# A transformer block on one core: TensorE's local program padded to whole blocks of 256 instructions, shorter packets for a value copy, new step orders

## The reference

```python
def attn_layer(x, Wqkv, qs, ksc, Wo):
    qkv = x @ Wqkv
    q, k, v = jnp.split(qkv, 3, -1)
    ...
    q = l2norm(q) * qs
    k = l2norm(k) * ksc
    ...
    q = q * cos * scale + rotate_half(q) * sin * scale
    k = k * cos * inv + rotate_half(k) * sin * inv
    out = local_attention(q, k, v)      # windows of 32: own and previous, softmax
    return out @ Wo

def ffn_layer(x, g, bln, W1, b1, W2, b2):
    ...
    a, gate = jnp.split(xn @ W1 + b1, 2, -1)
    return a * jax.nn.gelu(gate, approximate=False) @ W2 + b2
...
for i in range(DEPTH):                  # 6
    x = attn_layer(shift_tokens(x), Wqkv[i], q_scale[i], k_scale[i], Wo[i]) + x
    x = ffn_layer(shift_tokens(x), ln_g[i], ln_b[i], W1[i], b1[i], W2[i], b2[i]) + x
```

## Time and profile before

| | |
|---|---|
| median of 3 runs | 3510.96 us (3510.58 to 3515.58) |
| span of the profiled execution | 3495.1 us |
| local stage, first to last `lb` | 799.7 to 3467.5 us |
| PE busy | 3309.7 us (95%) |
| POOL busy | 2907.1 us (83%) |
| DVE busy | 2951.4 us (84%) |
| ACT busy | 2468.4 us (71%) |
| DMA queues' share | 40.9% |

### The profile page before, as it was taken

How to read it: one execution, slowest core, us unless ns; L and a number is a source line. 1 busy time by engine, 2 the same in 40 slices (tenths; PEclk the granted TensorE clock), 3 DMA queues, 4 the chain that set the end, 5 groups by cost and what they waited for, 6 DMA issues and landing times.

```text
span 3495.1 us, 158019 instructions
## 1 busy us (share of the span) xinstructions
PE 3309.7 (95%) x69988; PEld 1936.2 (55%) x69988; DVE 2951.4 (84%) x3104; ACT 2468.4 (71%) x3349; POOL 2907.1 (83%) x2483
## 2 busy tenths in 40 slices
PE   7999999779999999999999999999999999999997
PEld 4666666445555555555555555555555555555553
DVE  6888888688888988888888889888998889988873
ACT  5777777556777767777677777676877777767764
POOL 3665555588999989999899999898999999989993
PEclk9999999999999999999999999999999999999997
DMA  1000000154645545545455454555554554545452
GB/s 67 5 5 5 5 5 5 44 119 102 143 114 130 120 115 126 131 112 127 113 126 127 106 137 110 129 120 121 120 135 105 142 124 109 140 108 134 102 124 62
DMA packets 163861, 347.33 MB, mean 99 GB/s; under 512 B 32876, under 2 KB 42352, under 8 KB 153840
## 3 DMA queue, kind: packets, MB, share of 16 engines
q1 hardware_dynamic: 163184, 337.23, 40.9%
HBM read 24.62 MB, written 4.19 MB: 8 GB/s over the span
## 4 chain that ended last, share of the span: by engine, by line
PE 70%; DVE 11%; POOL 6%; issue 6%; ACT 4%; SPq 2%; DMA 1%; DVEq 0%; POOLq 0%; ACTq 0%
PE psA L697 29%; PE psB L697 23%; PE psB L559 8%; PE psA L559 6%; PE psB L754 3%; DVE h L1338 3%; DVE pt L1237 1%; SPq L490 1%; PE psA L754 1%; DVE negm L1342 1%; DVE sum L1349 1%; DVE ts L1330 1%; DVE h L1320 1%; DMA kf<-h 1%; POOL sq L1443 1%
## 5 line engine op out<-in xcount | busy, mean ns | idle before, releaser
L1410 POOL TENSOR_TENSOR pt<-wk,pt 128x256 f16<-128x256 f32 (+3 forms) x256 | 368.1, 1455 | 288.7 <-ACT pt L939 199.0
L1443 POOL TENSOR_TENSOR sq<-sq 128x512 f32<-128x512 f32 x384 | 488.5, 1281 | 79.6 <-ACT sq L1022 78.2
L1438 POOL TENSOR_TENSOR h<-h,ts 128x512 f32<-128x512 f32 x384 | 499.8, 1302 | 1.2 <-DVE ts L1330 1.2
L1439 POOL TENSOR_TENSOR h<-h,ts 128x512 f32<-128x512 f32 x384 | 497.1, 1295 | 0.0
L1338 DVE TENSOR_TENSOR h<-h,psB 128x1024 f32<-128x1024 f32 x288 | 337.8, 1215 | 57.1 <-PE psB L697 55.5
L1463 POOL TENSOR_TENSOR pb<-pb,rc 128x1024 f32<-128x1024 f32 x192 | 366.3, 1908 | 8.8 <-DVE rc L1351 8.8
L1320 DVE TENSOR_TENSOR h<-psA,t_rot 128x1024 f32<-128x1024 f32 x192 | 234.2, 1220 | 72.7 <-ACT sq L1022 65.7
L697 PE MATMUL psA<-kf,qf 64*32 64x64 f32 x18432 | 251.2, 224 | 22.0 <-issue 21.6
L697 PEld LDWEIGHTS psA<-kf,qf 64*32 64x32 f32 x18432 | 191.5, 106 | 124.8 <-issue 124.4
L1320 DVE TENSOR_TENSOR h<-psB,t_rot 128x1024 f32<-128x1024 f32 x192 | 233.4, 1216 | 26.2 <-ACT sq L1022 20.4
L1022 ACT ACTIVATE sq<-psA 128x1024 f32<-128x1024 f32 x192 | 197.0, 1027 | 63.7 <-PE psA L697 63.5
(11 more groups left out here) (368 smaller groups left out, 10242.0 us busy)
## 6 DMA issues: line engine op xcount, KB each, us to landing
qf<-h SPq DMA_DIRECT2D x768, 136.0 KB
kf<-h SPq DMA_DIRECT2D x768, 136.0 KB, 2.5
vev<-vo SPq DMA_DIRECT2D x288, 256.0 KB
vev<-vo SPq DMA_DIRECT2D x96, 192.0 KB
stage<-wqk SPq DMA_DIRECT2D x24, 256.0 KB, 5.0
stage<-wvl SPq DMA_DIRECT2D x12, 256.0 KB, 4.1
stage<-wof SPq DMA_DIRECT2D x12, 256.0 KB, 5.5
xb<-xt SPq DMA_DIRECT2D x8, 256.0 KB, 7.9
```

The source lines that it names most:

```text
L1410: e.tensor_tensor(pt[g][pr][:, :, 1, o:o + w], wk[(slot_of(s)[0] - 1) % SLOTS][:, :, 0:w], pt[g][pr][:, :, 0, o:o + w], ALU.subtract).then ...
L1438: e.tensor_tensor(halves_of(h, 0), halves_of(h, 0), t[1], ALU.subtract)
L1439: e.tensor_tensor(halves_of(h, 1), halves_of(h, 1), t[0], ALU.add).then_inc(ended["ad"])
L1443: e.tensor_tensor(sqb[c][:, 0, :], sqb[c][:, 0, :], sqb[c][:, 1, :], ALU.add).then_inc(ended["qa"])
```

## The change

It has four parts.

1. **Padding.** `local_tensor` counts its instructions (`issued`, from a start value LEAD of 76). Behind every `lb` it adds waits on `s_masks`, a semaphore that has long had its value, two to an instruction, until the count is a multiple of 256. In the built program 40 of the 48 batches get 28 to 32 of these wait instructions, five (the first batch of layers 2 to 6) get 7, the first two 167 and 51, the last two 70 and 74. From one `lb`'s padding to the next are then 2560 instructions.
2. **No repeated waits.** `need` leaves a wait out where TensorE has already waited for that value. In a steady batch 18 wait instructions are left beside the padding, where 38 stood. For the reader of a `pj` or `la` buffer the later one of its two readers in the walk is now waited for.
3. **Packets.** A row of `vev` gets 8 unused words at its end, so that the copy from `vo` breaks up into pieces of 2048 bytes. The DMAs are the same number and bytes.
4. **Orders.** All five strings are new.

```diff
 TENSOR = (
-    "pv000:B+1 ng10+1 pv001+1 ss1:Dl+1 sc110:A+1 tp01:C+1 sc113+1 sc111+1 sc112+1 pj00:B+2 pv010:D+1 ng11+1 pv011+1 "
...
+    "ss0:Al+3 pj10:D+3 sc000:A+3 sc002+3 sc003+3 sc001+3 op:Bl+2 ng00+3 sc010:C+3 bc00:D+3 sc013+3 sc011+3 sc012+3 "
...
-LAST = {"tp": "te", "op": "rs", "pj": "ts", "ss": "nr", "vp": "ve", "la": "lw",
-        "lb": "ln", "f": "fm", "fo": "fr"}
+LAST = {"tp": "te", "op": "rs", "ss": "nr", "vp": "ve", "lb": "ln", "f": "fm", "fo": "fr"}
...
+BLOCK, LEAD = 256, 76
...
-        vev = sb("vev", [128, NT, 2, 4, DH])
+        vev_rows = sb("vev", [128, NT, 2 * 4 * DH + 8])
+        vev = vev_rows[:, :, 0:2 * 4 * DH].rearrange("p t (f x d) -> p t f x d", f=2, x=4)
...
+        def later(steps, a, b):
+
+            return max(a, b, key=steps.index)
...
         def local_tensor(e):
+            at_block, waited, open_waits = [LEAD], {}, [0]
+
+            def need(semaphore, value):
+                if waited.get(semaphore.name, 0) < value:
+                    waited[semaphore.name] = value
+                    open_waits[0] += 1
+                    e.wait_ge(semaphore, value)
+
+            def issued(n):
+                at_block[0] += n + open_waits[0] // 2
+                open_waits[0] = 0
+
             def mm(o, l, r, start=True, stop=True, **kw):
+                issued(4 if r.dtype == F32 else 2)
                 return e.matmul(o, l, r, start=start, stop=stop, skip_group_check=True, **kw)
...
+                    elif k == "pj":
+                        need(*done(*later(vector_walk, ("tc", *at), ("ts", *at))))
+                    elif k == "la":
+                        need(*done(*later(scalar_walk, ("lq", *at), ("lw", *at))))
                     else:
-                        e.wait_ge(*done(LAST[k], *at))
+                        need(*done(LAST[k], *at))
...
                     p.then_inc(ended["lb"])
+                    while at_block[0] % BLOCK:
+                        e.wait_ge(s_masks, 1)
+                        e.wait_ge(s_masks, 1)
+                        issued(1)
```

More of the change, by code:

```diff
@@ L703, in take @@
                     if k == "bc":
-                        e.wait_ge(*all_done("bm", *((at[0], 2 * at[1] + x) for x in range(2))))
+                        need(*all_done("bm", *((at[0], 2 * at[1] + x) for x in range(2))))
                     elif k == "sc":
-                        e.wait_ge(*done("ex", *at[:2]))
+                        need(*done("ex", *at[:2]))
                     elif k == "pv":
-                        e.wait_ge(*done("ol", *at[:2]))
+                        need(*done("ol", *at[:2]))
+                    elif k == "pj":
+                        need(*done(*later(vector_walk, ("tc", *at), ("ts", *at))))
+                    elif k == "la":
+                        need(*done(*later(scalar_walk, ("lq", *at), ("lw", *at))))
                     else:
-                        e.wait_ge(*done(LAST[k], *at))
+                        need(*done(LAST[k], *at))
                 return psum(s)
@@ L741, in local_tensor @@
                     o = psum(("sc", v, rp, 0))
-                    e.wait_ge(*done("mx", v, rp))
+                    need(*done("mx", v, rp))
                     for x in range(2):
@@ L749, in local_tensor @@
                     o = take(s)
-                    e.wait_ge(*done("pn", v, rp))
+                    need(*done("pn", v, rp))
                     for x in range(2):
@@ L753, in local_tensor @@
                             at = 512 * x + 128 * t
+                            issued(2)
                             p = e.transpose(o[:, at:at + 128], pbs[rp][:, x, t, :], ident)
@@ L759, in local_tensor @@
                         o = take(s)
-                        e.wait_ge(*done("vd", v))
-                        e.wait_ge(*done("te", v, rp))
+                        need(*done("vd", v))
+                        need(*done("te", v, rp))
                     o = psum(("pv", v, rp, 0))
@@ L775, in local_tensor @@
                     o = take(s)
-                    e.wait_ge(*all_done("ol", *((2 * v + hf, rp) for hf in range(2) for rp in range(2))))
+                    need(*all_done("ol", *((2 * v + hf, rp) for hf in range(2) for rp in range(2))))
                     if v % NB == 0:
-                        e.wait_ge(*all_done("ow", (v - 1, 0), (v - 1, 1)))
+                        need(*all_done("ow", (v - 1, 0), (v - 1, 1)))
                     for i in range(8):
@@ L789, in local_tensor @@
                     o = take(s)
-                    e.wait_ge(*done("xl", v // 2))
+                    need(*done("xl", v // 2))
                     if b == 0:
-                        e.wait_ge(*done("wl", v // 2 - 1, half, c // 2))
+                        need(*done("wl", v // 2 - 1, half, c // 2))
                     x = [xs[b % 2][z][:, :] for z in range(2)]
@@ L806, in local_tensor @@
                     o = take(s)
-                    e.wait_ge(*all_done("qa", *((v, c) for c in range(4))))
+                    need(*all_done("qa", *((v, c) for c in range(4))))
                     for b in range(2):
@@ L815, in local_tensor @@
                     o = take(s)
-                    e.wait_ge(*done("ct", v))
+                    need(*done("ct", v))
                     for b in range(2):
@@ L825, in local_tensor @@
                     o = take(s)
-                    e.wait_ge(*done("xl", v // 2))
+                    need(*done("xl", v // 2))
                     if b == 0:
-                        e.wait_ge(*done("wl", v // 2 - 1, half, 2))
+                        need(*done("wl", v // 2 - 1, half, 2))
                     for c in range(2):
@@ L840, in local_tensor @@
                     o = take(s)
-                    e.wait_ge(*done("lq", v))
+                    need(*done("lq", v))
                     p = mm(o[:, 0:512], mean, f_a[:, :])
                     if v % NB == 0:
-                        e.wait_ge(s_w1, 16 * (li + 1))
+                        need(s_w1, 16 * (li + 1))
                         vl = V_LAYER + 10 * li
@@ L856, in local_tensor @@
                     if v % NB == 0:
-                        e.wait_ge(*done("wf", v - 1, 1))
-                    e.wait_ge(*done("fl", v))
+                        need(*done("wf", v - 1, 1))
+                    need(*done("fl", v))
                     for x in range(2):
@@ L868, in local_tensor @@
                     if v % NB == 0:
-                        e.wait_ge(*done("ws", v - 1, 1))
+                        need(*done("ws", v - 1, 1))
                     if v < final:
-                        e.wait_ge(*all_done("gl", *((v, j) for j in range(3))))
+                        need(*all_done("gl", *((v, j) for j in range(3))))
                     for i, j in enumerate(range(3) if v < final else [t[2] for t in last_low]):
```

14 lines of the change are left out of this document (7 added, 7 removed), and 23 rows, old and new, of tables (SCALAR, TENSOR, VECTOR).

## The result

The changed kernel takes 3702.32 us (median of 4 runs, 3683.21 to 3708.28) against 3513.27 us (4 runs, 3510.58 to 3521.09): a ratio of 1.0529, 95% interval 1.0501 to 1.0558 (the medians as they stand give 1.0538). The direction was the likelier one of the forecast; the size was outside its range of 3455 to 3575 us, 174 us above the forecast of 3528.

A forecast was written before the change was run, and what follows sets the result against it. PE was taken to set the pace, busy 95% of the span. Terms 92 + 16 - 25 - 51 - 15 + 0 = +17 us gave a span of 3512, with 15.9 us outside 3528 us; range 3455 to 3575.

The forecast's parts named there:

- padding, steady batches: Behind `lb` in 40 fully padded batches: 3.4 us of passed waits, 1.05 covered, 2.3 us idle each; +92 us (24 to 136).
- ends: Padding behind the first two and last two `lb`: about 9, 4, 3 us and hidden; +16 us (4 to 28).
- fetch stops: PE's stops at instruction-block boundaries, fixed by padding, fall from 1.3 to 0.8 us a period; -25 us (-60 to 0).
- denser steps, fewer waits: New step order and waits left out on PE save 1.1 us a period; -51 us (-23 to -62).
- waits for others: PE's waits for other engines, mainly at layer changes, shrink; -15 us (-30 to +50).
- packets: Value copy's shorter packets, with bytes, DMAs and issues unchanged, cost nothing; 0 us (-8 to +5).
- four tight blocks: Of a period's ten blocks, four hold 3.4 to 4.0 us of steps against 3.9 to 4.0 needed: about 0.8 us of stops.
- The 15.9 us outside the span: Profiled span of 3495.1 us lay 15.9 us below the median; added to the forecast span of 3512.
- Free padding: Rival: PE stands behind `lb` anyway or a passed wait costs little over 51 ns; 3460 us, chance 0.20.
- better orders that leave no stops: Rival: no fetch stops left, 1.35 us of denser steps, half the layer changes gone; 3472 us, chance 0.13.
- late copies of `qf` and `kf`: Rival: score sets come too early and PE waits for these copies, one us a period; 3574 us, chance 0.15.
- a pace set by POOL: Rival: POOL's chain with ScalarE sets a period of about 56.4 us, padding and gains cancel; 3511 us, chance 0.09.

The follow-up runs named there:

- 13: Changed kernel with padding only where at most 40 instructions are needed, so none at its ends; ratio 1.0440 to the kernel before.
- 2: Changed kernel with the value copy's target rows unpadded again, so packets are 8192 bytes; ratio 1.0480 to the kernel before, 3667 us.
- 8: Changed kernel with the value copy cut to 256 bytes a row, same DMAs, waits and block boundaries; ratio 1.0282 to the kernel before.
- 4: Changed kernel with the padding behind `op` instead of `lb`, start value 221; ratio 0.9955 to the kernel before, 3484.5 us.
- 9: As 4, but no padding where more than 40 instructions would be needed (none at the ends), start value 229; ratio 0.9837 to the kernel before.
- 14: Kernel before, old orders, with repeated waits left out, padding behind `op`, none at the ends, start value 142, long packets; ratio 0.9937 to the kernel before.
- 5: Kernel before with only the five new orders (and the later-reader wait they need), no padding, every wait kept, 8192-byte packets; ratio 1.0128.
- 10: Changed kernel with no waits behind `lb`, all 32 behind `op`, none at the ends, start value 109; ratio 0.9908 to the kernel before.
- 11: Changed kernel with 20 passed waits behind `lb`, 12 behind `op`, none beyond that, start value 129; ratio 0.9890 to the kernel before.

## Why the prediction was wrong

By its own steps, for the stage and its ends; what the runs showed, between the two profiled executions, is in the last column. The clock's term and what is left are rough.

| term | forecast | shown |
|---|---|---|
| padding, steady batches | +92 | +85 (39 x 2.19) |
| ends | +16 | +34 (13) |
| fetch stops | -25 | +34 (55 to 89) |
| clock | no term | about +100 |
| denser steps, fewer waits | -51 | -37 (46 x 0.8) |
| waits for others | -15 | about -5, what is left |
| packets | 0 | some 17 (2), within the stops and the clock |
| span | +17 | +211 |

**Padding: right.** The stop of 2.28 us, its place, its cover and its price by the piece. Only the count is one too high: 2 + 39 + 5 + 2 batches are 48, so 39 have a full padding, not 40.

**Fetch stops: the step that failed first.** "A block of 256 costs at least 3.7 to 4.3 us", whatever else goes on. Of my four tight blocks three had next to no stop, and the fourth, "`f`, `pv` and most of a `pv`, 3.8", had 2.05 us in the mean, because the value copy made its fetch late (8); it lasted 6.6 us. There is no fixed floor downward either: of the blocks that end in a stop some last 2.5 us in the kernel before and 2.4 us in 4, from PE's start to PE's start, others 4.3; and in the changed kernel one of 3.69 us ends without. A drift spreads a bad meeting over the periods; fixing the boundaries without looking at what the DMA engines do at each makes it happen in nearly all of them. I had looked at DMA only for the packets. (46 x 0.5 is 23 and not 25, which changes nothing.)

**Clock: a missing term.** PE's busy time is 104 us longer than in 9, with the same matmuls. The mean clock says the same: (1 - 0.957) x 3706.5 = 159 us of full speed lost, against (1 - 0.987) x 3446.5 = 45. Before, it was 49. I had read "1.00" and "0.97" in the earlier trace rows, with PE busy 2.8 us more in the 0.97 row, and asked nothing of it. The stops of the stage, 83 us at the value copy and 112 behind the `lb`s, came with these 104 us of slower work: half as much again.

**Denser steps: right in kind, too large.** 1.1 us a period was 0.8. PE's busy time of a period at full clock went from 55.05 to 54.25 us in the mean (29 periods of before, 28 of 9). With the old orders and the waits left out (14) it is 54.70: the waits are worth some 0.35, the orders 0.45. But alone the orders lose (5): what they do to the blocks outweighs it.

**Ends: too small.** I let others make up for 6 of the 15 us behind the first `lb` and took 13 us for the first two periods; they are 27.6 us longer than in 13, in part because PE ran at 1.2 GHz for 23.9 us around that stop. The period before the last `lb` is 10.8 us longer, where I had 3. The padding behind the last `lb` was hidden, as forecast.

**The 15.9 us outside the span were no such thing.** In every execution since, the time is 1.7 to 3.0 us above its span (mostly 1.8); the one profiled before lies 14 us below the median of its kernel. The forecast doesn't change by it: 17 us on top of the median, 3511, are 3528 too.

**The rivals.** Free padding, better orders that leave no stops, late copies of `qf` and `kf` (6.2 us in 16 waits from 862 to 3300), a pace set by POOL: none happened. The first two are what 9 shows to be possible in another place. The Trainium skill, page "Runtime: NRT & Kernel Launch", section "Instruction fetch mechanics", has the fetch hidden; the trace again does not agree: 83 us of stops in one place, gone when the bytes of the value copy went (8).

## What to carry to other kernels

A list of steps can hide passed waits only behind work that PE already has in its queue: behind `op`, 24 matmuls of 512 columns, 32 of them were free (4, 9), behind `lb` they cost 2.3 us each time. It holds only while no block boundary falls into that work: in 10 one did, and they cost 1.0 us behind `op` too. Whoever fixes where instruction blocks begin should lay those places beside the DMA timeline as well as beside dense steps, for what meets once meets in nearly every period. A stop of 2.3 us added to a dense TensorE stream should be priced with the slower clock behind it, here half as much again.

## What the hardware showed that I had not expected

- The fetch of the next 256 instructions can be held up by data DMAs, and not by all alike. With the value copy cut down (8) it started 1.3 us after its block. With that copy of 960 KB still moving at the block's start it started 3.9 us after it (3.3 with 8192-byte pieces), 2.4 us after the copy's last piece had ended, and the block lasted 6.6 us. Amid the copies of queries and keys (before) it started after 1.6 us. How the value copy does it is not shown.
- TensorE's clock fell to 1.2 GHz behind many of the stops of some 2.3 us (about half of them), mostly for 3.4 to 10.2 us, 51 stretches and 319 us in all, against 17 and 98 us before; with stops of 0.93 us (11) there were 11 stretches and 71 us, fewer than before.
- A passed wait takes TensorE's sequencer 0.105 us (median from one to the next) behind `lb` and behind `op` alike; only the work in PE's queue decides whether PE stands for it.
